# A two-layer graph network on one core: the layer norm of x moved to ScalarE and GpSimd, the destination table loaded first, and the ring's places given back by TensorE

## The reference

```
h = relu(layernorm(x))
x = x + relu(h @ W_self + mean_over_in_edges(h[src]) @ W_neigh + b)          # layer 0
h = relu(layernorm(x))
hid = relu(concat(h[src], h[dst]) @ We1 + be1)                               # per edge
m   = sigmoid(hid @ We2 + be2) * h[src]
m_sum, m_max = segment_sum(m, dst), segment_max(m, dst)                      # per node
x = x + relu(concat(m_max, m_sum, h) @ Wn1 + bn1) @ Wn2 + bn2 + h            # layer 1
```

## Time and profile before

| | us |
|---|---|
| three runs | 7823.34, 7826.61, 7837.4 |
| median | 7826.61 |
| profiled execution, its device time | 7808.26 |
| its span, first to last instruction | 7806.6 |
| busy: PE, DVE, ACT, POOL | 2274.1, 4104.2, 2785.0, 3649.8 |
| mean granted TensorE clock | 0.646 |

### The profile page before, as it was taken

How to read it: one execution, slowest core, us unless ns; L and a number is a source line. 1 busy time by engine, 2 the same in 40 slices (tenths; PEclk the granted TensorE clock), 3 DMA queues, 4 the chain that set the end, 5 groups by cost and what they waited for, 6 DMA issues and landing times.

```text
span 7806.6 us, 104387 instructions
## 1 busy us (share of the span) xinstructions
PE 2274.1 (29%) x18241; PEld 1987.1 (25%) x18241; DVE 4104.2 (53%) x8571; ACT 2785.0 (36%) x7197; POOL 3649.8 (47%) x3826
## 2 busy tenths in 40 slices
PE   0006855555555555551000001101111111111110
PEld 0005855555555555551000000000000000000110
DVE  5774844444444444440055655656666655666672
ACT  5104744444444444441023333333333333333341
POOL 5232033333333333336655555555555555555545
PEclk9998977777777777775555555555555555555555
DMA  8110332222222222224433333333333333333332
GB/s 230 34 24 19 43 90 92 84 84 84 85 84 84 84 84 85 84 87 134 140 77 91 91 93 89 98 91 98 97 93 91 93 91 91 102 99 98 107 102 40
DMA packets 491278, 696.09 MB, mean 89 GB/s; under 512 B 249885, under 2 KB 339843, under 8 KB 491163
## 3 DMA queue, kind: packets, MB, share of 16 engines
q0 software_dynamic: 181472, 381.28, 17.8%
q1 hardware_dynamic: 228085, 172.05, 7.2%
q10 hardware_dynamic: 81638, 141.95, 5.8%
HBM read 513.68 MB, written 163.18 MB: 87 GB/s over the span
## 4 chain that ended last, share of the span: by engine, by line
issue 33%; ACTq 16%; PE 15%; another core or an unknown queue 13%; ACT 11%; DVE 9%; DVEq 1%; POOL 1%; DMA 0%; POOLq 0%; SPq 0%
PE ps L1835 7%; PE ps_acc L1843 7%; ACTq L1702 6%; ACT msg L1702 5%; ACT counts_f L1603 3%; DVE act_w L1436 3%; ACT gate L1697 2%; ACTq L1753 2%; ACTq L1697 2%; DVE run_max L1453 1%; ACTq L1770 1%; DVE z L1442 1%; POOL out_dram L706 1%; ACTq L1669 1%
## 5 line engine op out<-in xcount | busy, mean ns | idle before, releaser
L572 POOL DMA_INDIRECT counts_f<-hA_table,stage x2144 | 2053.2, 958 | 1764.6 <-issue 622.0
L1603 ACT ACTIVATE counts_f<-ps 128x784 bf16<-128x784 f32 x1568 | 1261.7, 822 | 1920.9 <-remote 945.9
L1702 ACT ACTIVATE msg<-counts_f,gate (+1 forms) x3448 | 967.2, 338 | 1110.7 <-issue 880.7
L1835 PE MATMUL ps<-hot 128*128 128x196 bf16 x6272 | 918.2, 275 | 1180.9 <-ACT counts_f L1603 743.0
L1843 PE MATMUL ps_acc<-pieces_f,counts_f 128*128 128x192 bf16 x9604 | 1178.2, 270 | 1.7 <-issue 1.0
L572 POOL DMA_INDIRECT extra_f<-hA_table,estage x984 | 932.3, 947 | 310.9 <-issue 310.9
L1843 PEld LDWEIGHTS ps_acc<-pieces_f,counts_f 128*128 128x128 bf16 x9604 | 1015.7, 143 | 8.8 <-issue 1.9
L1272 DVE TENSOR_TENSOR hot<-ps_t,iota_lo 128x2048 bf16<-128x2048 bf16 x392 | 479.6, 1223 | 1023.0 <-remote 791.0
L1914 PE MATMUL ps_acc<-ident,h_tile 128*64 128x128 f32 x98 | 38.6, 394 | 3172.3 <-ACT h_tile L1714 1717.4
L1835 PEld LDWEIGHTS ps<-hot 128*128 128x128 bf16 x6272 | 597.0, 107 | 1316.7 <-issue 1280.2
L1430 DVE TENSOR_TENSOR pre<-counts_f,ps 128x512 f32 (+1 forms) x862 | 587.7, 682 | 612.2 <-issue 453.1
(11 more groups left out here) (230 smaller groups left out, 2851.5 us busy)
## 6 DMA issues: line engine op xcount, KB each, us to landing
early_rows<-extra_f SPq DMA_DIRECT2D x294, 384.0 KB
counts_f<-early_rows ACTq DMA_DIRECT2D x98, 1152.0 KB
counts_f<-hA_table,stage POOLq DMA_INDIRECT x2144
counts_f<-counts_f SPq DMA_DIRECT2D x67, 288.0 KB
extra_f<-hA_table,estage POOLq DMA_INDIRECT x984
own<-own_rows ACTq DMA_DIRECT2D x98, 130.0 KB
hA_table<-node ACTq DMA_DIRECT2D x98, 96.0 KB
ranked_rows<-zeros SPq DMA_DIRECT2D x1, 3724.0 KB
```

The costliest lines, as they stand in the source:

```text
L572: return pool.indirect_dma_start(to, None, table, bass.IndirectOffsetOnAxis(ap=idx, axis=axis))
L1603: act.activation(counts[:, c, nodes, :].rearrange("p (b h) t -> p b (h t)", h=2), ps_pairs[g & 1][:, :].rearrange("p (b w) -> p b w", b=BA ...
L1702: last = act.activation(msg[:, bass.ds(w & 1, 1), s, :].rearrange("p a d -> p (a d)"), rows[:, s, 0:D], ACT.Copy, scale=gate[:, bass.ds(w ...
L1835: last = pe.matmul(ps_pairs[g & 1][:, i * (BANK // 2):i * (BANK // 2) + 2 * T], hot_lo[:, (g // 4) & 1, at // 2, :, at % 2], hot_hi[:, (g ...
```

## The change

**The table first.** SP broadcasts `dst_top` before it loads x, and holds the two zero transfers back until the search has ended (`s_start`). The table and two scratch areas move to other buffers.

**The layer norm of x.** The 14 halves on DVE go. In seven of the search's iterations DVE computes `bn_stats` of 14 tiles each (98 in all), and from them the mean and the variance in five operations on 128x98. ACT takes one square root; DVE a reciprocal and one product. ACT makes h with 98 Relu activations, scale and bias from the statistics, copies it to the first piece (14 copies) and stores it. POOL, behind its last gather of `runs`, takes two subtractions of 128x3136, ACT two copies, POOL two further subtractions for the pieces. DVE waits for the 14 first pieces before `near` and for the last subtractions before the one-hot.

**Layer 1.** ACT loses its waits `done`, the loop and the give-backs. PE walks over the tiles with registers of its own, waits for the messages and gives the places back: loop after b+3 ahead of `hidden`, 4 places after b+4 ahead of `output`, 4 after b+5, and then those of the inner loop.

```diff
@@ SP
             sp.dma_start(dst_top[:], dst_rows[:, 0:1]...).then_inc(s_topd, 16)
+            sp.wait_ge(s_topd, 16)
+            sp.dma_start(top_i[:, :], dst_top[:].unsqueeze(0).to_broadcast([P, TOP])).then_inc(s_top, 16)
             sp.wait_ge(s_zero, 2)
             sp.dma_start(x_nodes[:, 0:FULL, :], ...)
             sp.dma_start(x_nodes[0:REST, FULL, :], x[FULL * P:N, :]).then_inc(s_x, 16)
-            sp.wait_ge(s_topd, 16)
-            sp.dma_start(top_i[:, :], dst_top[:].unsqueeze(0).to_broadcast([P, TOP])).then_inc(s_top, 16)
...
+            sp.wait_ge(s_start, 1)
             sp.dma_start(extra_rows..., zeros...)
             sp.dma_start(ranked_rows..., zeros...)
@@ POOL
+            pool.wait_ge(s_first, 2 * TITER)
+            for h in range(2):
+                half = slice(h * (T // 2), (h + 1) * (T // 2))
+                pool.tensor_tensor(x_nodes[:, half, :], h_nodes[:, half, :], pieces[:, half, 0:D], ALU.subtract
+                                   ).then_inc(s_rest, 1)
+            for h in range(2):
+                pool.wait_ge(s_sec, h + 1)
+                pool.tensor_tensor(pieces[:, half, 2 * D:3 * D], x_nodes[:, half, :], pieces[:, half, D:2 * D],
+                                   ALU.subtract).then_inc(s_piece, 1)
@@ DVE
+                    if tiles is not None:
+                        for k in range(a * MTILES // PARTS, (a + 1) * MTILES // PARTS):
+                            v.bn_stats(at_tile(moments, tiles + k), at_tile(x_nodes, tiles + k))
                     count(it, a)
...
+            v.wait_ge(s_first, 2 * TITER)
             for s in range(EPIECES):
                 st.link(v.tensor_scalar(near, ...))
...
             v.wait_ge(s_h0w, H0_DMAS)
+            v.wait_ge(s_piece, 2)
             st.link(v.tensor_tensor(onehot, ...))
@@ ACT
+            act.activation(cols3[:, :], cols2[:, :], ACT.Sqrt, bias=eps_col[:, 0:1], scale=1.0 / D).then_inc(s_std, 1)
+            act.wait_ge(s_norm, 1)
             with in_one_block(act, 0, 2 * TITER) as g:
+                for k in range(THALF):
+                    last = act.activation(at_tile(h_nodes, g * THALF + k), at_tile(x_nodes, g * THALF + k), ACT.Relu,
+                                          scale=cols3[:, one], bias=early_n[:, one])
+                last.then_inc(s_h0, 1)
+                act.activation(pieces[:, tiles_at, 0:D], h_nodes[:, tiles_at, :], ACT.Copy).then_inc(s_first, 1)
...
-                if before_it is not None:
-                    act.sem_inc(l1.used, SLOTS)
...
-                done(before + ECHUNKS)
-                with act.Fori(0, first_late(slots)):
-                    act.sem_inc(l1.used, 1)
...
-                done(before + (ECHUNKS + 1))
-                act.sem_inc(l1.used, SLOTS)
...
-                        done(w - 1)
-                        act.sem_inc(l1.used, SLOTS)
@@ PE
-            with in_one_block(pe, 0, T) as i:
-                sum_transposes(i)
-                hidden(i)
-                output(i)
+            def free(w, n):
+                wait_alone(pe, s_msg, w + 3)
+                pe.sem_inc(l1.used, n)
+            def tile(i, before_it):
+                slots, slots_before, n, before = walk.tile()
+                if before_it is not None:
+                    sum_transposes(before_it)
+                wait_alone(pe, s_msg, before + (ECHUNKS + 3))
+                with pe.Fori(0, first_late(slots)):
+                    pe.sem_inc(l1.used, 1)
+                if before_it is not None:
+                    hidden(before_it)
+                free(before + (ECHUNKS + 1), SLOTS)
+                if before_it is not None:
+                    output(before_it)
+                free(before + (ECHUNKS + 2), SLOTS)
+                walk.go_on(...)
+                with pe.If(n > ECHUNKS + 3):
+                    with pe.Fori(ECHUNKS + 3, n) as c:
+                        free(before + c, SLOTS)
```

More of the change, by code:

```diff
@@ L234, in gnn_kernel @@
         rows_sb = extra_f[:, :].bitcast(I32).rearrange("p (t k) -> p t k", k=RUN)
-        near = counts_f[:, 0:T * EARLY].rearrange("p (t k) -> p t k", k=EARLY)
+        near = hot_b[:, 0:2 * T * EARLY].bitcast(F32).rearrange("p (t k) -> p t k", k=EARLY)
         onehot_flat = counts_f[:, T * D:T * D + BINS * T]
@@ L330, in gnn_kernel @@
         own_f = own[:, :, :].rearrange("p a w -> p (a w)")
[L331 to L332 removed]
+        top_i = own_f[:, 0:TOP].bitcast(I32)
+        moments = runs[:, :, :, :].rearrange("p h t k -> p (h t k)")[:, 0:6 * T].bitcast(F32).rearrange(
+            "p (t m) -> p t m", m=6)
         key = pre[:, :, :].rearrange("p s h -> p (s h)")[:, 0:THALF * WINDOW].rearrange("p (t k) -> p t k", k=WINDOW)
@@ L393, in gnn_kernel @@
         s_h0w = sem("s_h0w")
+        s_norm = sem("s_norm")
+        s_first = sem("s_first")
+        s_rest = sem("s_rest")
+        s_sec = sem("s_sec")
+        s_piece = sem("s_piece")
         s_degf = sem("s_degf")
@@ L987, in _ @@
             v.tensor_scalar(thr[:, :], thr[:, :], (READY[0] + 1) * P - 0.5, None, ALU.add).then_inc(s_thr, 1)
[L989 to L1008, removed]
-                st.link(v.tensor_tensor(rest_1[:, :, :], h_nodes[:, tiles_at, :], first, ALU.subtract))
-                st.link(v.tensor_copy(second, rest_1[:, :, :]))
-                st.link(v.tensor_tensor(third, rest_1[:, :, :], second, ALU.subtract))
-            v.wait_ge(s_x, X_DMAS)
-            first, per = st.now(), 10 * 2
-            with in_one_block(v, 0, TITER) as it:
-                st.at(it * per + first)
-                for h in range(2):
-                    first_h(bass.ds(it * (2 * THALF) + h * THALF, THALF), it * 2 + h + 1)
-                assert st.n == per, st.n
-            st.at(first + per * TITER)
             v.wait_ge(s_thrb, 1)
@@ L1776, in tile @@
                     messages_of(act.snap(before + n), early_rows_of(next_it, 0))
-                    done(before + n)
             act.activation(ps_we2, we2_rows[:, :], ACT.Copy).then_inc(s_second, 1)
@@ L1928, in output @@
                 pe.matmul(ps_y[:, 0:D], ident[:, :], own_at(i, X_AT, H_AT), start=False, stop=True).then_inc(l1.y, 1)
-            with in_one_block(pe, 0, T) as i:
-                sum_transposes(i)
-                hidden(i)
-                output(i)
+            def free(w, n):
[14 more added lines that the diff above has]
+                free(before + (ECHUNKS + 2), SLOTS)
+                walk.go_on(slots, slots_before, n, before, i + 1 if not isinstance(i, int) or i < T - 1 else None)
+                with pe.If(n > ECHUNKS + 3):
+                    with pe.Fori(ECHUNKS + 3, n) as c:
+                        free(before + c, SLOTS)
+            walk = Walk(pe, "walk_pe")
+            tile(0, None)
+            with in_one_block(pe, 1, T - 1) as i:
+                tile(i, i - 1)
+            tile(T - 1, T - 2)
+            sum_transposes(T - 1)
+            hidden(T - 1)
+            output(T - 1)
 _INS = ['x', 'src', 'dst', 'L0_gnn_W_self', 'L0_gnn_W_neigh', 'L0_gnn_b', 'L1_gnn_We1', 'L1_gnn_be1', 'L1_gnn_We2',
```

52 lines of the change are left out of this document (37 added, 15 removed).

## The result

| | before, us | changed, us | ratio |
|---|---|---|---|
| first comparison | 7824.98 | 8111.81 | 1.0366 (1.0348 to 1.0384) |
| second comparison, later | 7805.62 | 8106.24 | 1.0386 (1.0361 to 1.0411) |

The changed kernel is 287 us slower. The direction was forecast; the size, +46, was not, and 8112 lies outside the range of 7738 to 7985. The stages of the changed kernel, in the columns of the earlier trace rows: the end of the search to the start of the sort, the sort up to the classes, and layer 1.

A forecast was written before the change was run, and what follows sets the result against it. It took layer 1 to be bound by a chain through several engines, paying for ACT's latency. Stages ahead of layer 1 at -90 us and layer 1 at +136 made +46: 7872 us, range 7738 to 7985.

The forecast's parts named there:

- Part 1: Start: the table's cast on DVE, and ACT's search behind it, come earlier, -11.5 us.
- Part 2: Search: 98 bn_stats on DVE cost +18 us after 4.3 of cover, small operations +2.5.
- Rival B: Search: DVE's added register instructions stretch to 0.7 us, +94 us, 7966 in all; chance 0.10.
- Part 3: Between search and sort: the layer norm stage goes, the sort starts 12.5 us after the search, -105.3 us.
- Parts 4 and 5: Sort: zero transfers now beside its first gathers, +3 us; Pool's four subtractions mostly covered before the one-hot, +3 us.
- Part 6: Layer 1: PE and ACT take turns, +1.4 us a tile, +136 us in all, bounds 0 and +245.
- The delay of +2.7: Layer 1: the gate of b+5 comes 2.7 us later in each tile, counted from a tile taken as usual.
- The -1.0 for a lighter ACT: Layer 1: instructions leaving ACT save 2.0 us a tile in its slow stretch, half counted, -1.0.
- The -0.3 that DVE was allowed: Layer 1: DVE has a little time in hand to absorb the delay, -0.3 us a tile.
- The 0 for give-backs that come earlier: Layer 1: places given back 1 us and more earlier change nothing, since gathered rows are not waited for.
- A: Layer 1: the delay is absorbed and the lighter ACT decides, 7736 us or 7640 in all; chance 0.26.
- C: No change: layer 1 loses 0.9 us a tile, +90, and the prologue gives it back, 7827 us; chance 0.12.

The follow-up runs named there:

- ab_only: Changed kernel with layer 1 as in the kernel before: 7731.89 us, ratio 0.9923 to the kernel before, with stretched instructions.
- ab_split: ab_only with Pool's four subtractions cut into 28 pieces: 5435.71 us against 5497.36 for the kernel before, without stretched instructions.
- ab_best: ab_only with zeros at the start and 28 subtraction pieces spread between Pool's gathers: 5407.38 us against the kernel before's 5497.54, without stretched instructions.
- c_pe_first2: Kernel before plus the layer 1 change alone, PE's hidden and output ahead of its waits: 5492.54 us against 5497.54, without stretched instructions.
- c_again: Kernel before plus the layer 1 change alone: 5801.99 us against 5496.35 for the kernel before, without stretched instructions.
- c_pe_first: Kernel before plus the layer 1 change alone, PE's hidden and output ahead of its waits: 8048.7 us, ratio 1.0319, with stretched instructions.
- pe_dummy4: Kernel before plus PE's walk, waits and loops adding to a semaphore nobody waits for: 7868.22 us against 7805.62, with stretched instructions.

## Why the prediction was wrong

**Part 1, the start: right.** -11.5 was forecast, the cast came 12.8 us earlier (14.50 against 27.33).

**Part 2, the bn_stats: mis-sized, by 15 us.** With the earlier start the search should have ended 9 us later than before; it ended 7.7 earlier. The 98 bn_stats and the small operations together cost 12.8 - 7.7 = 5 us and not 20.5. The working counted only the 4.3 us put down to a DMA as cover; the "issue" idle time of DVE was cover as well. In the changed kernel's search the counts have 3.1 us of idle time before them and not the 17.2 of the earlier trace rows:

```profile
L961 DVE TENSOR_SCALAR_CACHE_REDUCE hot<-extra_f,q_node 128x625 bf16<-128x625 int32 x100 | 82.5, 864 | 3.1 <-issue 1.4 <-DMA extra_f<-in_dst_dram,sstage 1.0 <-DVE hot L961 0.4
```

Rival B, in which DVE's register instructions would stretch the search, did not come.

**Part 3: right,** -102.8 against -105.3. The sort's first step came 15.0 us behind the search's end and not 12.5; the seventh gather begins six steps of 1.25 us behind the first, 7.5 and not 8.75, so the true gap to the working is a little wider.

**Parts 4 and 5: the durations were right and the conclusion wrong.** Pool's subtraction was taken as 4.4 to 13.8 us and took 6.1, four of them 24.4, less than the cover of 30.6 us. But the working asked only who waits for Pool, and not whom Pool holds while it works: DVE stood still in the cover that was to hide them, for 25.08 us. That is half of the sort's +49. The other 24 us lie in its first four halves: 197.64 to 265.8 in the changed kernel, 308.10 to 352.8 before. The largest pieces are idle times of DVE that the profile puts down to "remote", to nothing on this core, the longest 8.93 us before L1052 at 209.84 (in ab_only 7.3). The zeros and the stores of h are under way then, but that they are the cause is not shown: ab_split writes the zeros at the same place, on a chip without stretched instructions, and its first two halves take as long as in ab_best, where the zeros stand at the start. There only some 7 us hang on the zeros. The two terms had been +3 each.

**Part 6, layer 1: the mechanism was right, its size and its cover were wrong.** The step "PE and ACT now take turns" is shown by c_pe_first2 against c_again. The working for the first tile was near: the gate of b+5 at +9.3, measured +10.5 in c_again's tile. What failed is the sum of +1.4 us a tile; 366 / 97 = 3.8 was measured.

- The delay of +2.7 was a little small. The tile taken as the usual one was usual: its gate of b+5 at +6.7 is the kernel before's median of 6.8 (mean 7.7). But in the new order the gate stands at +10.6 in the median and not at +9.3. A pass of PE's loop was put at 0.3 us and takes 0.7, so `hidden` starts at +1.7 behind two passes and not at +0.8; and PE's output starts 0.6 us behind the end of the messages b+4 (3992.89 and 3993.53 in c_again's tile), for which the working had nothing. By the means the delay is 10.8 - 7.7 = 3.1 us, by the medians 3.8.
- What was taken off it did not come. The -1.0 for a lighter ACT was a guess: with the turns gone (c_pe_first), the kernel with the lighter ACT was 250 us slower on a chip with stretched instructions, and 5 us faster on one without. The -0.3 that DVE was allowed did not come either: with the mean delay of 3.1 the tile grew by 3.8. By the means, 0.4 of the 2.4 us that the sum missed lie in the delay, and 2.0 here.
- The 0 for give-backs that come earlier did not hold in c_pe_first, where 190 us go with their move. In the changed kernel itself there are 92 rows of 4 gathers and 80 of 12 or 16, hardly other than before.
- The upper bound of 245 us was worked out from the chosen tile, 97 x 2.5 (which is 242.5), and so left out the quick tile's 3.8 that the text had itself derived (97 x 3.8 = 369, the measured 366 within it). The upper bound of -45 for the stages ahead of layer 1 is not the sum of its terms' upper bounds either: -11.5 + 45 + 2.5 - 105.3 + 15 + 25 = -29; the measured -59 lay inside both.

**The rivals.** A, that the delay is taken up in ACT's long stretch: no, layer 1 grew in every kernel with the turns, on both sorts of chip. C: no.

**The sum.** -59 + 366 for -90 + 136. Layer 1 missed by 230 us, the stages ahead of it by 31.

## What to carry to other kernels

When bookkeeping is moved to an idle engine, look at what stands behind each new wait in that engine's program: PE was 11% busy in layer 1, and four lines in another order would have made the move free on chips without stretched instructions (-5 us and not +306). Put the products that another engine waits for first and the bookkeeping last. When work is moved to GpSimd, check DVE's operations under it one by one, since a hold shows up as a long busy instruction and not as a wait; spread such work out between other instructions of GpSimd, and expect short holds in place of the long one (11 us and not 28 here). Before an added pause is read as one, look in the trace whether anything moved apart. And when an upper bound is worked out, take it from the worst tile seen, not from the one chosen as usual.

## What the runs showed of the hardware

The same kernel takes 7800 us on some chips and 5497 on others, each to within some 0.3%. On the first, register, branch and semaphore instructions of ACT are stretched to 0.7 us and more while Pool's gathers run, in L1702 up to 1414 ns against 106: of 1255 such instructions of ACT in layer 1 of the kernel before, 1169 begin within 1 us of a row of gathers, and the rows fill 2632 of 3801 us. DVE has 145, SP 89 and PE none, but PE has 50 in pe_dummy4. Gathers in a row are not enough for it: on the others c_pe_first2 has 1784 of them in one row, and no such instruction of ACT reaches 0.5 us. There layer 1 is for long stretches bound by Pool's gathers; between 3000 and 3100 us of c_pe_first2 the chain of work that ended last reads

```profile
by line: POOL counts_f L572 71.8%; issue 27.5%; POOLq L537 0.7%; POOLq L538 0.3%; POOLq L686 0.3%
```

What stretches the instructions is open. The Trainium skill (Runtime: NRT & Kernel Launch, section Instruction fetch mechanics) puts a stall on a taken branch whose target is not in the fetched window; here plain register instructions in a straight line are stretched as well (862 of the 1255 have no branch among themselves and the four before them), and on some chips only. PE's added loops cost 60 us on such a chip with nobody waiting for them.
